# The first 512-token tile of a gated feed-forward kernel with gathered low-rank corrections: worked by token halves, with first loads and DVE steps in another order

## What is computed

```python
def lora_add(base, inp, A, B):
    Ab = A[layer_idx][lora_indices]
    Bb = B[layer_idx][lora_indices]
    t = jnp.einsum('bri,bni->bnr', Ab, inp)
    return base + jnp.einsum('bor,bnr->bno', Bb, t) * SCALE
gate = lora_add(jnp.einsum('bnh,fh->bnf', x, W_gate), x, A_gate, B_gate)
up = lora_add(jnp.einsum('bnh,fh->bnf', x, W_up), x, A_up, B_up)
act = jax.nn.silu(gate) * up
down = lora_add(jnp.einsum('bnf,hf->bnh', act, W_down), act, A_down, B_down)
...
x_abs_max = jnp.clip(jnp.max(jnp.abs(x), axis=-1, keepdims=True), EPS)
out = jnp.einsum('bsd,od->bso', x / x_abs_max, QUANT_LEVELS[weight_2bit])
out = out * (x_abs_max * weight_scale) + bias
x = x + ffn(cond(x))
```

## Time and profile before

| | |
|---|---|
| median of 3 runs | 922.29 us (921.65 to 923.16) |
| the profiled execution's own time | 923.06 us |
| its span, first to last instruction | 921.1 us |
| PE busy | 888.0 us, 96% of the span |
| PE weight loads busy (beside the matmuls) | 715.6 us |
| DVE, ACT, GpSimd busy | 349.0, 260.5, 81.9 us |
| DMA | 45.38 MB, mean 49 GB/s |

### The profile page before, as it was taken

The page is one execution under the profiler, slowest core; times in us unless marked ns, Lnnn a source line. Parts: engine busy times, 40 slices in busy tenths (PEclk is TensorE's granted clock), DMA queues, the critical chain, the costliest instruction groups (busy, mean ns, idle before and its releaser), DMA issues.

```text
span 921.1 us, 13664 instructions
## 1 busy us (share of the span) xinstructions
PE 888.0 (96%) x3930; PEld 715.6 (78%) x3930; DVE 349.0 (38%) x754; ACT 260.5 (28%) x448; POOL 81.9 (9%) x110
## 2 busy tenths in 40 slices
PE   2999999999999999999999999999999999999994
PEld 2778888888888887888888888888888888888873
DVE  3564345222642334422353324432254223542223
ACT  2442243111522124211242213411152222422112
POOL 0011003010030000300003100021003000201200
PEclk9899999999999999999999999999999999999998
DMA  3555121111112011120111102111111111210001
GB/s 96 141 171 174 33 61 36 44 34 30 42 42 55 23 35 49 29 67 11 49 47 38 46 13 54 54 37 34 31 46 46 49 29 32 58 32 25 12 15 49
DMA packets 45445, 45.38 MB, mean 49 GB/s; under 512 B 13168, under 2 KB 31984, under 8 KB 45392
## 3 DMA queue, kind: packets, MB, share of 16 engines
q1 hardware_dynamic: 43024, 41.85, 16.8%
q10 hardware_dynamic: 2368, 3.02, 1.2%
HBM read 36.44 MB, written 8.39 MB: 49 GB/s over the span
## 4 chain that ended last, share of the span: by engine, by line
PE 92%; SPq 2%; DMA 2%; DVE 2%; ACT 1%; issue 1%; DVEq 0%; ACTq 0%
PE pw_up L1705 25%; PE pw_down L1749 23%; PE pw_gate L1705 23%; PE ps_misc L1774 6%; PE pw_td L1738 4%; PE pw_down L1759 2%; PE pw_up L1715 2%; PE ps_misc L1705 2%; PE pw_gate L1715 2%; PE ps_misc L1766 1%; DMA wb_raw<-b_rows 1%; SPq L570 1%; DMA rows<-w_down 0%; DMA plan_room<-places 0%; SPq L307 0%
## 5 line engine op out<-in xcount | busy, mean ns | idle before, releaser
L1749 PE MATMUL pw_down<-wd,wact_split 128*128 128x512 f32 x960 | 232.5, 391 | 0.0
L1705 PE MATMUL pw_up<-wxs,wgu 128*128 128x512 f32 x948 | 229.4, 391 | 0.0
L1749 PEld LDWEIGHTS pw_down<-wd,wact_split 128*128 128x128 f32 x960 | 180.2, 188 | 44.5
L1705 PE MATMUL pw_gate<-wxs,wgu 128*128 128x512 f32 x864 | 211.4, 393 | 1.6 <-ACT wact_full L994 1.5
L1705 PEld LDWEIGHTS pw_up<-wxs,wgu 128*128 128x128 f32 x948 | 178.4, 188 | 38.6
L1705 PEld LDWEIGHTS pw_gate<-wxs,wgu 128*128 128x128 f32 x864 | 160.0, 188 | 35.1 <-issue 2.4
L1355 DVE TENSOR_TENSOR wact_full<-pw_up,wact_full 128x512 f32<-128x512 f32 (+1 forms) x87 | 60.0, 690 | 296.5 <-PE pw_up L1715 294.3
L994 ACT ACTIVATE wact_full<-pw_gate 128x512 f32<-128x512 f32 (+1 forms) x80 | 47.9, 599 | 276.2 <-PE pw_gate L1715 276.2
L1006 ACT ACTIVATE wact_split<-wact_full 128x512 fp32r<-128x512 f32 x80 | 50.5, 631 | 69.7 <-DVE wact_full L1355 69.7
L1360 DVE TENSOR_TENSOR wact_split<-wact_full,wact_split 128x512 fp32r<-128x512 f32 x80 | 55.7, 696 | 26.4 <-ACT wact_split L1006 26.3
L800 POOL TENSOR_TENSOR rows<-rows,bias 128x512 f32<-128x512 f32 x28 | 35.8, 1290 | 222.5 <-DMA rows<-x_tok 221.3
(11 more groups left out here) (119 smaller groups left out, 668.2 us busy)
## 6 DMA issues: line engine op xcount, KB each, us to landing
out<-rows SPq DMA_DIRECT2D x120, 64.0 KB, 1.6
rows<-x_tok SPq DMA_DIRECT2D x112, 64.0 KB, 1.8
rows<-w_gu SPq DMA_DIRECT2D x8, 512.0 KB, 4.3
x_raw<-x_feat SPq DMA_DIRECT2D x60, 64.0 KB, 1.8
x_more<-x_feat SPq DMA_DIRECT2D x60, 64.0 KB, 1.8
wb_raw<-b_rows SPq DMA_DIRECT2D x32, 92.0 KB, 2.9
low_room<-b_rows SPq DMA_DIRECT2D x32, 80.0 KB, 2.5
rows<-w_down SPq DMA_DIRECT2D x9, 256.0 KB, 4.2
```

Of the source, the lines that this page charges most:

```text
L1705: last = nc.tensor.matmul(bank, w, wxs[:, xp, k, :], start=(n == 0 and k == 0), stop=False, skip_group_check=(f == 0))
L1749: last = nc.tensor.matmul(pw_down[:, s, :], wact(ap, f)[:, s * P:(s + 1) * P], wd[:, wp, f, :], start=(f == 1 and n == 0), stop=False)
```

## The change

The diff, cut to what matters:

```diff
@@ the first tile on PE
+            def half_pass(bank, f, g, n, half):
+                ws, xp = PASSES[n]
+                tokens = slice(half * TILE, (half + 1) * TILE)
+                for k in range(KC):
+                    w = wgu_first[:, ws, k, g, :] if f == 0 else wgu_chunk(ws, f)[:, k, g, :]
+                    last = nc.tensor.matmul(bank[:, tokens], w, wxs[:, xp, k, tokens],
+                                            start=(half == 0 and n == 0 and k == 0), stop=False,
+                                            skip_group_check=True)
+                return last
+
+            def first_tile_chunks():
+                pe.wait_ge(wgu_lo, 1)
+                pe.wait_ge(a_ready, 1)
+                for half in range(2):
+                    pe.wait_ge(x_hi, half + 1)
+                    for n in range(3):
+                        if n == 2:
+                            pe.wait_ge(x_lo, half + 1)
+                        gate = half_pass(pw_gate, 0, 0, n, half)
+                        up = half_pass(pw_up, 0, 1, n, half)
+                        if n == 2 and half == 1:
+                            gate.then_inc(t_done, 1)
+                            up.then_inc(t_done, 1)
+                    if half == 0:
+                        pe.wait_ge(wgu_lo, 2)
+                    for n in range(3):
+                        half_pass(ps_misc, 1, 0, n, half)
+                    for n in range(3):
+                        half_pass(up_bank(1, True), 1, 1, n, half)
@@ ACT, wide_tile
-                for half in range(2):
-                    wide_x_hi(tile, half, first)
+                wide_x_hi(tile, 0, first)
+                if first:
+                    for e in range(FROM_ACT, ENTRIES):
+                        load_x_entry(act, wide_place(0, ENTRIES + e), x_more[:, e, :], x_more_in)
+                wide_x_hi(tile, 1, first)
                 if first:
                     load_wgu(act, 2)
                     load_wd(act, 0)
                     load_wd(act, 1)
-                    split_hi_wgu(2)
                     wide_b_hi(tile, 0, first)
                     wide_b_hi(tile, 1, first)
+                    split_hi_wgu(2)
                     wide_t_hi(tile, 0)
                     wide_t_hi(tile, 1)
                     split_hi_wd(0)
@@ ACT, wide_program
-                for e in range(1, ENTRIES, 2):
-                    load_x_entry(act, wide_place(0, ENTRIES + e), x_more[:, e, :], x_more_in)
@@ ACT, start of the program
+            act.dma_start(number_places, places).then_inc(index_in, 16)
+            for f in range(2):
+                load_wgu(act, f)
             act.wait_ge(ones_ready, 1)
             nc.scalar.activation(rinv[:, 0:1], ones[:, :], ACT.Silu)
-            for f in range(2):
-                load_wgu(act, f)
             split_hi_wgu(0)
             split_hi_wgu(1)
-            act.wait_ge(plan_steps, PLAN_ORDER_STEP)
-            load_a(act, lora_at(act, wide_place(0, WENTRIES - 1)), first_a[:, 1, :], first_a_in)
+            act.wait_ge(plan_listed, 1)
@@ SP, wide_program, and its start
+                for e in range(0, FROM_ACT):
+                    load_x_entry(sp, wide_place(0, ENTRIES + e), x_more[:, e, :], x_more_in)
                 idx = wide_loras(0)
-                for e in range(0, ENTRIES, 2):
-                    load_x_entry(sp, wide_place(0, ENTRIES + e), x_more[:, e, :], x_more_in)
-                load_mask(0, mask_gu, mask_gu_in)
-                wide_b(idx, 0)
-                wide_ad(idx, 0)
+                load_wide_b(sp, idx, 0)
+                load_mask(sp, 0, mask_gu, mask_gu_in)
+                load_wide_ad(sp, idx, 0)
...
             sp.dma_start(idx_places, lora_index).then_inc(index_in, 16)
-            sp.dma_start(number_places, places).then_inc(index_in, 16)
-            sp.wait_ge(plan_steps, PLAN_ORDER_STEP)
-            load_a(sp, lora_at(sp, wide_place(0, 0)), first_a[:, 0, :], first_a_in)
+            sp.wait_ge(plan_listed, 1)
@@ GpSimd, start of the program
+            pool.wait_ge(plan_listed, 1)
+            for slot, e in enumerate((0, WENTRIES - 1)):
+                load_a(pool, lora_at(pool, wide_place(0, e)), first_a[:, slot, :], first_a_in)
@@ DVE, wide_tile
                 if first:
-                    split_lo_wgu(2)
                     wide_b_lo(tile, 0)
                     wide_b_lo(tile, 1)
-                    for g, bank in enumerate((pw_gate, pw_up)):
-                        wide_mask_t(tile, g, bank, first)
-                        wide_t_lo(tile, g)
+                    wide_mask_t(tile, 0, pw_gate, first)
+                    wide_mask_t(tile, 1, pw_up, first)
+                    wide_t_lo(tile, 0)
+                    wide_t_lo(tile, 1)
+                    split_lo_wgu(2)
                     split_lo_wd(0)
@@ DVE, make_plan: plan_listed goes up with the last copy into plan (L1501)
+                        copied = nc.vector.tensor_copy(plan[row:row + 1, 0:BATCH // 2]
...
+                copied.then_inc(plan_listed, 1)
```

More of the change, by code:

```diff
@@ L60 @@
 WARM_UP = 24
+FROM_ACT = 3
 PLAN_COLUMNS_STEP = 8
-PLAN_ORDER_STEP = 9
 WQ_FROM = FC - KC
@@ L195, in build @@
         plan_gathered = sem("plan_gathered")
+        plan_listed = sem("plan_listed")
         plan_ready = sem("plan_ready")
@@ L352, in store, with load_wide_b, load_wide_ad, first_run @@
                                   out_rows[at:at + SEQ, s, :]).then_inc(stored, 16)
+        def load_wide_b(eng, idx, piece):
+            a, b = piece_columns(piece)
+            dst = (wb_raw[:, 0:b - a], b_second[:, 0:b - a])[piece]
+            for copy in range(2):
+                for e in range(2):
+                    at = copy * PAIR + e * RANK
+                    eng.dma_start(dst[at:at + RANK, :], b_rows[bass.ds(idx[e], 1), :, a:b]
+                                 .rearrange("a r n -> (a r) n")).then_inc(b_in[piece], 16)
+        def load_wide_ad(eng, idx, piece):
+            f0, f1 = PIECES[piece]
+            for e in range(2):
+                eng.dma_start(wad_raw[:, e, f0 * RANK:f1 * RANK],
+                             a_down[bass.ds(idx[e], 1), :, f0 * RANK:f1 * RANK].rearrange("a p n -> (a p) n")
+                             ).then_inc(ad_in[piece], 16)
+        def first_run(eng, tile):
+            return eng.value_load(plan_run[:, bass.ds(tile, 1)], min_val=0, max_val=WENTRIES)
+        def load_mask(eng, tile, dst, done):
+            eng.dma_start(dst, pair_masks[bass.ds(first_run(eng, tile), 1), :, :].rearrange("a p n -> (a p) n")
+                         ).then_inc(done, 16)
         def store_wide(eng, tile, s, entries=range(SUB_ENTRIES)):
@@ L1500, in make_plan @@
                         row = first_row + 32 * half
-                        nc.vector.tensor_copy(plan[row:row + 1, 0:BATCH // 2]
-                                              .rearrange("p (t e) -> p t e", t=TILES), by_half[:, :, half, :])
+                        copied = nc.vector.tensor_copy(plan[row:row + 1, 0:BATCH // 2]
+                                                       .rearrange("p (t e) -> p t e", t=TILES),
+                                                       by_half[:, :, half, :])
+                copied.then_inc(plan_listed, 1)
                 then(nc.vector.tensor_copy(sorted_idx, ps_plan[32:33, :]))
@@ L1711, in wide_main, with wide_lora, wide_first_chunk @@
                     wide_pass(bank, f, g, n)
-            def wide_lora(tile, bank, f, g, done):
+            def wide_lora(tile, bank, f, g, done, halves=False):
                 w = WIDTHS[f]
                 nc.tensor.matmul(bank[0:w, :], wb_split[0:STACK, f % 2, g, 0:w], wt_split[0:STACK, g, :],
-                                 start=False, stop=True, skip_group_check=(f == 0)).then_inc(done, 1)
-            def wide_first_chunk(tile, first):
-                if not first:
-                    pe.wait_ge(act_done, FC * tile)
-                else:
-                    pe.wait_ge(wgu_lo, 1)
+                                 start=False, stop=True, skip_group_check=(f == 0 or halves)).then_inc(done, 1)
+            def wide_first_chunk(tile):
+                pe.wait_ge(act_done, FC * tile)
                 pe.wait_ge(x_hi, 2 * tile + 2)
@@ L1797, in wide_tile @@
                 pe.wait_ge(b_lo, FC * tile + 2)
-                wide_lora(tile, ps_misc, 1, 0, gate_done)
+                wide_lora(tile, ps_misc, 1, 0, gate_done, halves=first)
                 if not first:
@@ L1802, in wide_tile @@
                     wide_main(pw_up[:, :], 1, 1)
-                wide_lora(tile, up_bank(1, first), 1, 1, up_done)
+                wide_lora(tile, up_bank(1, first), 1, 1, up_done, halves=first)
                 for f in range(2, FC):
```

62 lines of the change are left out of this document (20 added, 42 removed).

## The result

The changed kernel takes 916.87 us, the median of four runs (915.53 to 917.62), beside 922.7 us for the kernel before (four runs, 921.65 to 923.16): the ratio is 0.9942, with a 95% interval of 0.9931 to 0.9954. That is 5.3 us faster by the ratio and 5.8 us by the medians, where 7.9 us were forecast. Its profiled execution took 916.88 us with a span of 914.9 us, 6.2 us under the 921.1 us before.

The account below looks back on a forecast made before the run. PE sets the pace from chunk f = 3 on, so an earlier start reaches the end: low-rank matmuls 8.5 us earlier, 0.6 us given back, 922.29 - 7.9 = 914.4 us; 913.4 to 915.5 us by small terms, 912.9 to 917.3 us with rivals.

Parts of the forecast that it names:

- The first chain: Start of the kernel up to chunk f = 3: `places` lands, the plan, x requested entry by entry, x split, PE.
- PE by halves: PE's first tile: 96 matmuls of 256 columns at 0.117 us, straight after the warm-up, costing 0.4 us in all.
- late A matrices: Rival, GpSimd's loads at the start: slow or held up by DVE, about 2 us lost, 916.4 us; 25%.
- a late plan: Rival, at the start: `places` still lands at 5.2 us, 1.7 us less gain, 916.1 us; 7%.
- I take 3.5 us: Start of the plan: later of `places` and index table lands at 3.5 us, bounds 3.2 and 5.2 us.
- The A matrices: GpSimd's loads at the start: second matrix lands at 12.7 us, covered with 0.5 us to spare.
- lands at 20.9 us: First tile's load of x: ACT's last request of the second half at about 19.1 us, landed at 20.9 us.
- landed 4.3 us later: ACT's path to the low-rank matmuls: `w_gu` of f = 2, requested at 20.9 us, lands at 25.2 us.
- `w_gu` sooner: Rival, ACT's path: with B out of its way `w_gu` lands in 3.5 us, 913.6 us; 8%.
- I expect no fall of the clock: PE's first tile: the idle stretch of 6.4 us closes, so the granted clock stays high.
- f = 3 starts at 30.8 + 11.34: Start of chunk f = 3: SP released at 30.8 us, f = 3 11.34 us later at 42.1 us.
- 0.6 us given back: DVE ahead of SP's release: `wgu` subtraction of f = 2 now between t and `wd`, losing 0.6 us.

Follow-up runs that it names:

- e3: The changed kernel with SP asking for `w_gu` of f = 3 only once that of f = 2 has landed; 913.63 us, ratio 0.9917.
- e4: The changed kernel with 14 idle matmuls of 256 columns added on PE ahead of the low-rank matmuls; 915.02 us, ratio 0.9931.
- e1: The changed kernel with PE's halves undone: first tile as 48 matmuls of 512 columns behind both splits of x; 920.09 us, ratio 0.9982.
- e2: The changed kernel with SP asking for B, mask, A_down and `w_gu` of f = 3 only once x's second half has landed; 920.15 us, ratio 0.9982.
- e5: The changed kernel with DVE's `w_gu` subtraction of f = 2 put ahead of the two t subtractions; 916.46 us, ratio 0.9939.
- e8: The changed kernel itself, run again beside the kernel before; 916.35 us, ratio 0.9944.
- e9 to e11: The changed kernel, x's second half four entries per queue: `w_gu` of f = 3 held back; alone; held back with `w_gu` subtraction first; 915.23, 915.52, 915.65 us.

## Why the prediction was right and where it was wrong

The first chain (plan, x, PE by halves) and the sign were right. What failed are the landing times of the two loads on ACT's path, the clock that was to hold, and SP's release as what sets f = 3; the gain was sized 2.1 to 2.6 us too high. 916.87 us lies outside the 913.4 to 915.5 us of the forecast's own terms. It lies in the wider range up to 917.3 us by luck: that range was widened for late A matrices (916.4 us) and a late plan (916.1 us), and neither came. By its own steps:

- **"I take 3.5 us" for `places`**: it landed at 3.16 us, even below the lower bound of 3.2 us, and the rival in which the plan starts no earlier is out. SP's first request for x went out at 8.29 us (8.7 us forecast), and the first half was in at 13.97 us (13.8 us).
- **The A matrices**: GpSimd's two requests took 0.70 and 0.54 us, with a gap of 0.50 us between them, and the second landed 2.6 us after its issue, at 12.79 us (12.7 us forecast). The rival with a quarter of the chance didn't come either. POOL's timeline:

```profile
8.94 0.70 POOL L325 DMA_DIRECT2D first_a<-a_gu  x1 [7.87 <-issue]
10.14 0.54 POOL L325 DMA_DIRECT2D first_a<-a_gu  x1 [0.50 <-issue]
```

  DVE's subtractions ran from 8.99 to 11.1 us, right through both. The sentence of the Trainium skill, page "SBUF — State Buffer", section "Who interferes with whom", that such subtractions don't stop GpSimd's descriptors, agrees with this; there is no run without the subtractions to compare. The estimate of 2.15 us from the Trainium skill, page "DMA: Bandwidth & Descriptors", section "Anatomy of one DMA — SWDGE (gpsimd) path", was 0.5 us short of the 2.6 us measured.
- **PE by halves**: 0.12 us for a matmul of 256 columns, and no gap behind the warm-up, both right. The halves are not what brought the clock down: it held with them in e3 and e4. e1 puts the halves at 3.5 us.
- **"lands at 20.9 us" for x's second half** is the first step that failed: 22.47 us, 1.6 us late. The last request was on time, 19.16 us against 19.1 us. The 1.8 us to landing came from a stretch with little but x's own requests in it, while the same paragraph moved B's requests into this very stretch. e2 takes B out and the landing is at 20.70 us. This term of the sum was mis-sized: 3.3 us, not 1.8 us.
- **"landed 4.3 us later" for `w_gu` of f = 2** is the second: 5.3 us, 1.0 us late. I had B out of its way, and overlooked that the request for f = 3, 3.3 us behind it before, moves up to 0.4 us ahead of it. e3 holds that one back and the load of f = 2 lands in 3.9 us. With these two the low-rank matmuls are 2.6 us late, 31.5 instead of 28.9 us. The rival "`w_gu` sooner" had the sign wrong for the same reason.
- **"I expect no fall of the clock"** is the third. The idle stretch of 6.4 us closed, but the late chain opened two others, of 1.90 and 1.86 us, and the clock fell behind the second: 1.0 to 1.4 us by e4.
- **"f = 3 starts at 30.8 + 11.34"**: the release came at 33.30 us, and f = 3 10.4 us later. The 11.34 us held four requests for B's second piece, which now take 1.79 us and not 3.6. In e4 the stretch is 42.38 - 32.82 = 9.6 us, so SP's path had at least 0.8 us to spare, and the "0.6 us given back" by the DVE order wasn't on the path (e5). There was no stall ahead of f = 3, where 2.1 us were forecast. PE, at the low clock for part of the way, set the start of f = 3, 12.2 us behind the low-rank matmuls.

The sum: the forecast's 42.1 us, plus 2.6 us for the two landings, less 0.9 us for the shorter way from release to f = 3, is 43.8 us; measured are 43.69 us. The 0.9 us is itself taken from the measured start of f = 3, so this sum only shows where the difference sits. PE's own path, with numbers of other runs, is the test: 31.48 us, 11.2 us as in e4, and 4.14 - 3.01 = 1.1 us for twelve matmuls at the low clock, 43.8 us. Without the fall f = 3 would have started at some 42.7 to 42.9 us, an estimate from 31.48 + 11.2 us by PE's path and 33.30 + 9.6 us by SP's. So 1.6 us of the missing gain are in the profiles (43.69 against 42.1 us). The rest is that before's profiled execution lay 0.4 to 0.8 us above its median and the one after on it, so that of 6.2 us between the profiles 5.3 to 5.8 us are left.

Left open: e3 still has the first gap of 1.7 us. A version in which the mask is asked for ahead of B, with four and four entries, was not tried. Nor is settled what decides over the clock. It held behind a gap of 1.73 us with 0.49 us later (e3) and behind a single one of 1.01 us (e4), fell behind two of 1.6 and 1.6 us (e8) and of 1.34 and 1.89 us (e5), and fell within or behind single ones of 2.75 to 3.18 us (e9 to e11); in between nothing was measured.

## What to carry to other kernels

When a change moves a request, price it and its new neighbours for the stretch in which they will now be under way: a landing time from the old trace holds only with the company that it had there. List which request was behind which on every queue, those that no edit names too (here `w_gu` of f = 3, moved up without an edit, cost 2.3 us until it was told to wait for the load that was needed first). And when a gap on PE is closed by bringing data forward, look at what remains as several short gaps: the clock can be lost to them.
